# Moving nine FFN products from the output stage of the last phase into its scan loop

## The reference, cut to what matters

```python
xn = layernorm(x)
# branch 1: 16 states for each of 1024 channels, scanned over the tokens
delta = softplus(xn @ Wd.T + bd)
a_bar = exp(-delta * softplus(a_log))
state = a_bar * state + delta * b_param * xn      # over time
y     = state.sum(-1)
# branch 2
real = xn @ cos(theta + theta_noise)
imag = xn @ sin(phi + phi_noise)
out  = x + (y @ Wo.T + bo) + sqrt(real*real + imag*imag)
```

## Time and profile before

| what | value |
|---|---|
| median of the runs | 1132.94 us (2 runs, 1132.84 to 1133.04) |
| the profiled execution | 1131.38 us |
| its span, slowest core (core 3) | 1129.6 us; the eight cores 1123.7 to 1129.6 us |
| VectorE busy | 812.6 us (72%) |
| ScalarE busy | 587.2 us (52%) |
| TensorE busy | 583.5 us (52%) |
| mean granted TensorE clock, core 3 | 0.685 of full speed |

### The profile page before, as it was taken

The page is one execution under the profiler, slowest core; times in us unless marked ns, Lnnn a source line. Parts: engine busy times, 40 slices in busy tenths (PEclk is TensorE's granted clock), DMA queues, the critical chain, the costliest instruction groups (busy, mean ns, idle before and its releaser), DMA issues.

```text
span 1129.6 us, 9385 instructions; the slowest of 8 cores (1123.7 to 1129.6 us)
## 1 busy us (share of the span) xinstructions
PE 583.5 (52%) x2248; PEld 240.7 (21%) x2248; DVE 812.6 (72%) x725; ACT 587.2 (52%) x927; POOL 155.7 (14%) x132
## 2 busy tenths in 40 slices
PE   0423333344467645555544556665565554465685
PEld 0301011111123321221210213443221211121353
DVE  3359788888763348989889984334889989998423
ACT  4575766666643315665555553332465555655430
POOL 2577000000011200000000001221000000000232
PEclk9955555656668856666555666987766556665799
DMA  8877000000002310000000001231100000000023
GB/s 236 228 230 205 2 28 29 28 19 1 0 24 79 111 45 0 1 1 0 1 1 0 1 0 41 87 118 57 42 1 0 0 1 0 1 0 1 28 71 112
DMA packets 36326, 51.67 MB, mean 46 GB/s; under 512 B 3120, under 2 KB 19760, under 8 KB 36272
## 3 DMA queue, kind: packets, MB, share of 16 engines
q1 hardware_dynamic: 33584, 42.68, 13.1%
q0 software_dynamic: 2688, 8.39, 2.1%
HBM read 42.67 MB, written 8.39 MB: 45 GB/s over the span
## 4 chain that ended last, share of the span: by engine, by line
DVE 42%; issue 22%; PE 21%; ACT 10%; POOL 2%; DMA 1%; DVEq 1%; ACTq 0%; POOLq 0%; SPq 0%
DVE grot L722 34%; PE pd L845 6%; PE pt L569 4%; PE pt L579 3%; ACT bdg_bf L171 3%; PE pd L278 3%; DVE sfm L859 2%; ACT abar L676 2%; DVE gcar L733 1%; DMA xsub<-xin 1%; PE pe L357 1%; DVEq L111 1%; PE py L873 1%; ACT L676 1%; DVE xsub L419 1%
## 5 line engine op out<-in xcount | busy, mean ns | idle before, releaser
L722 DVE TENSOR_TENSOR_SCAN grot<-abar,gcar,vbuf 128x768 bf16<-128x768 f32 (+1 forms) x384 | 643.8, 1736 | 69.1 <-ACT abar L676 59.5
L676 ACT ACTIVATE abar<-delta,nega 128x768 f32<-128x768 f32 (+1 forms) x384 | 342.4, 898 | 272.0 <-DVE grot L722 269.0
L760 PE MATMUL pe<-grot,bdg_bf 128*128 128x384 bf16 x256 | 91.6, 460 | 124.8 <-DVE grot L722 124.7
L760 PE MATMUL py<-grot,bdg_bf 128*128 128x384 bf16 x256 | 88.2, 449 | 117.4 <-DVE grot L722 117.4
L278 PE MATMUL pd<-xnbf,wd_bf 128*128 128x384 bf16 (+1 forms) x368 | 97.6, 446 | 18.0 <-ACT xsub L297 14.6
L747 PE MATMUL py<-grot,bdg_bf 128*128 128x512 bf16 x64 | 33.3, 533 | 84.7 <-DVE grot L722 84.7
L619 POOL TENSOR_TENSOR xsub<-r,i 128x384 f32<-128x384 f32 (+1 forms) x9 | 18.1, 2009 | 410.5 <-ACT i L611 410.5
L845 PE MATMUL pd<-ybf,wo_bf 128*128 128x384 bf16 (+1 forms) x320 | 73.3, 379 | 0.0
L747 PE MATMUL pe<-grot,bdg_bf 128*128 128x512 bf16 x64 | 34.3, 543 | 74.9 <-DVE grot L722 74.9
L569 PE MATMUL pt<-xnbf,cos_bf 128*128 128x384 bf16 (+1 forms) x320 | 71.7, 374 | 0.0
L579 PE MATMUL pt<-xnbf,sin_bf 128*128 128x384 bf16 (+1 forms) x320 | 64.8, 347 | 0.0
(11 more groups left out here) (104 smaller groups left out, 565.3 us busy)
## 6 DMA issues: line engine op xcount, KB each, us to landing
xsub<-xin SPq DMA_DIRECT2D x14, 512.0 KB, 4.2
xres<-xin SPq DMA_DIRECT2D x32, 192.0 KB, 2.5
out<-osub POOLq DMA_DIRECT2D x32, 192.0 KB, 2.7
xres<-xin SPq DMA_DIRECT2D x8, 256.0 KB, 3.7
out<-osub POOLq DMA_DIRECT2D x8, 256.0 KB, 3.5
r<-wdt SPq DMA_DIRECT2D x6, 256.0 KB, 6.5
i<-wdt SPq DMA_DIRECT2D x6, 256.0 KB, 6.6
etmp<-tht SPq DMA_DIRECT2D x6, 256.0 KB, 4.5
```

The source lines that it names most:

```text
L676: sx = run("scalar", lambda e, sl=sl_ab, par=par, dt=dt, n=n, tp=tp: e.activation(out=abar[:, sl * TP:sl * TP + tp], in_=delta[:, par * TP ...
L722: vs = run("vector", lambda e, g=gsl, sl=sl_ab, par=par, dt=dt, n=n, tp=tp: e.tensor_tensor_scan(out=grot[:, g * TP:g * TP + tp], data0=ab ...
L760: td = run("tensor", lambda e, c=c, g=gsl, dt=dt, n=n, bb=ypair[c]: e.matmul(bb[:, 0:384], bdg_bf[:, (dt * NST + n) * P:(dt * NST + n + 1) ...
```

## The change

Only phase 2 (the last) changes. All 16 FFN jobs now run in its scan loop, two in each channel tile. Job 2·dt has its matmuls at the top of the tile as before. Its chain, the matmuls of job 2·dt+1 and the chain of that job are entries of `aux`, so they stand behind the exp of consecutive states: behind n = 7, 8 and 9 in tiles 1 to 6, behind n = 5, 6 and 7 in tile 0, and behind n = 3, 4 and 5 in tile 7 (whose `aux` has fewer other entries). The chain at the end of a tile is gone in this phase, and the output stage has no FFN work left. Since the ring's slots in `delta`, `vbuf` and `abar` are in use during the loop, jobs 5 to 15 put their results into `xn32` (the normalised input), into rows that the multiplications of line 333 have already read.

```diff
         NRING = len(ring_ap)
-        ring_stt = [0] * NRING
-        ring_g = [0] * NRING
+        ring_ap = ring_ap + [xn32[:, 512 * s:512 * s + 512] for s in range(12)]
+        ring_stt = [0] * (NRING + 12)
+        ring_g = [0] * (NRING + 12)
...
             def ring_avail_waits(j, eng):
+                if j >= NRING:
+                    s = j - NRING
+                    wait(eng, "V", a_x32_v[p])
+                    wait(eng, "S", a_xnbf_s[p])
+                    for r_ in range((512 * s) // TP, (512 * s + 511) // TP + 1):
+                        wait(eng, vv_done[r_][0], vv_done[r_][1])
+                    return
...
+            P2SLOT = {5: 3, 6: 5, 7: 0, 8: 1, 9: 2, 10: 4,
+                      11: 6, 12: 7, 13: 8, 14: 9, 15: 10}
+
+            def rslot2(i):
+                if p == NPH - 1 and i in P2SLOT:
+                    return NRING + P2SLOT[i]
+                return rslot(i)
...
-            ffn_at = ({6: [0], 7: [1]} if p == 0
-                      else {0: [0], 1: [1], 2: [2], 3: [3], 4: [4],
-                            5: [], 6: [5], 7: [6]})
-            NFC = 2 if p == 0 else 7
+            if p == 0:
+                ffn_at = {6: [0], 7: [1]}
+                NFC = 2
+            elif p == NPH - 1:
+                ffn_at = {dt_: [2 * dt_] for dt_ in range(NDT)}
+                NFC = nch
+            else:
+                ffn_at = {0: [0], 1: [1], 2: [2], 3: [3], 4: [4],
+                          5: [], 6: [5], 7: [6]}
+                NFC = 7
...
+                if p == NPH - 1:
+                    aux.append(("fch", 2 * dt, 0))
+                    aux.append(("fmm", 2 * dt + 1, 0))
+                    aux.append(("fch", 2 * dt + 1, 0))
...
+                        elif kind == "fmm":
+                            emit_ffn_mm(adt)
+                        elif kind == "fch":
+                            emit_ffn_chain(adt)
...
-                for jb in ffn_at.get(dt, []):
-                    emit_ffn_chain(jb)
+                if p != NPH - 1:
+                    for jb in ffn_at.get(dt, []):
+                        emit_ffn_chain(jb)
```

More of the change, by code:

```diff
@@ L596, in rslot @@
                 return i - NRING + 3
+            P2SLOT = {5: 3, 6: 5, 7: 0, 8: 1, 9: 2, 10: 4,
[4 more added lines that the diff above has]
+                return rslot(i)
             def emit_ffn_chain(i):
                 dt, c0, wdth = cjobs[i]
-                j = rslot(i)
+                j = rslot2(i)
                 li = i % 2
@@ L851, in _build @@
                 slot = it % 2
-                jr = rslot(it)
+                jr = rslot2(it)
                 wait("vector", "T", tw)
```

## The result

The changed kernel takes 1140.4 us (median) against 1133.1 before: ratio 1.0067, 95% interval 1.0057 to 1.0077. The ratio leaves out the few executions in which the cores of one die show a lower clock than the others and take longer. The forecast was 1143.5 us with a range of 1132 to 1158, and "within 2%" with a chance of 0.83. So the change makes the kernel slower, as forecast: by 7.3 us, or 0.7%, where 10.6 us, or 0.9%, were forecast.

A forecast was written before the change was run, and what follows sets the result against it. VectorE was taken to bound the phase 2 loop and TensorE the output stage. From 1131.4 us, +29.9 in the loop and −19.5 in the output stage gave 1141.8, or 1143.5 as median; range 1132 to 1158.

The forecast's parts named there:

- Both chains together, 5.15 a tile: Phase 2 loop, tiles 0 to 6: the two mid-tile chains delay scan 10, costing 5.15 us a tile, 36.1 in all.
- the base tile: Phase 2 loop: a tile without losses takes 29.96 us; eight, less 0.38, make 239.3 us.
- 5.68 for the block: Mid-tile in the loop: the second job's 16 matmuls end 5.68 us after scan 7, mostly at the lower clock.
- 4.07 for the rest: After that block: second square, add, Ln, Exp and abar take 4.07 us until scan 10 starts.
- The tile's top, 0.83 each: Start of tiles 1 to 6: VectorE waits for TensorE's states, 0.83 us each, 5.0 in all, between 0.04 and 1.49.
- Tile 7, 6.4: Last tile of the loop: chains at n = 3 to 5 with no vbuf multiplication to cover them lose 6.4 us.
- the 17.6 of before: Phase 2 loop of the kernel before: stalls worth 17.6 us for seven chains, over eight base tiles.
- The output stage: After the phase 2 loop: 54.7 us instead of 74.2, 19.5 shorter, pieces 2.76 apart, three products at the lower clock.
- The rival of a stage that stays at 1.2 GHz: Output stage: the other thirteen products run slow too, 1.31 us each, adding 17.0 for 1160.5 us; chance 0.12.
- The colliding adds: Phase 2 loop: the second add comes while VectorE scans without pause, adding 9.8 us for 1153.3; chance 0.10.
- Hidden altogether: Phase 2 loop: it hides the moved work and today's stalls go too, giving 1096 us, −3.3%; chance 0.03.

The follow-up runs named there:

- e5: Changed kernel with each phase 2 chain cut in two: squares behind one exp, Ln and Exp two states later; 1109.5 us, ratio 0.9786.
- e1: Changed kernel with each tile's second phase 2 chain three states later, its matmuls left in place; 1124.8 us, ratio 0.9935.
- e9: Changed kernel with one job per phase 2 tile, eight in the output stage, and the chain behind n = 12; 1129.0 us, ratio 0.9967.
- e4: Changed kernel with the first job's 16 matmuls moved from the top of tiles 1 to 6 to behind state 2; 1137.7 us, ratio 1.003.
- e10: The split-chain kernel e5 with GpSimd's additions of phase 2 left out; 1099.8 us, ratio 0.9705.
- e6: Changed kernel with three abar slots instead of two in all phases; 1124.9 us, ratio 0.9925, phase 2 loop 294.9 us.
- e2: Changed kernel with one job per phase 2 tile, chain behind n = 7 in tiles 1 to 6, and eight jobs in the output stage; 1134.7 us, ratio 0.9999.
- e8: The split-chain kernel e5 with e4's edit and phase 1's chains split too, all but job 5; 1097.6 us, ratio 0.9674.

## Why the prediction was right

The forecast held because its two terms did: +27.3 in the loop against a forecast of +29.9, and −20.0 in the output stage against −19.5. The mechanism is the forecast one; inside both terms, some smaller errors cancel.

**Both chains together, 5.15 a tile.** Right in place, cause and size: tiles 1 to 6 lost 36.1 us over the base tile, top and chains, against 35.9 in the forecast, and tile 0 lost 5.0 against 5.15. That the two chains share one loss which ends 9.75 after scan 7 was the step that carried it: scan 10 started 9.6 after scan 7's end in tile 4 (967.01 − 957.40), and 9.76 in the mean of tiles 1 to 6. Its two parts, 5.68 for the block and 4.07 for the rest, hold roughly, but only in every second tile. In tiles 2, 4 and 6 the block ended a microsecond earlier (4.70 in tile 4), and the add took a microsecond longer (1.86 to 1.97 instead of 0.98), as it came beside scan 9. The prediction had said in a sentence that these two would about cancel, and they did, within 0.4 us a tile. e5 beside e1 shows that a large part of the loss is ScalarE's standing for the adds, and e1 beside e9 that the wait for the second chain's matmuls is another.

**The tile's top, 0.83 each.** Right: 0.23 to 1.34, together 4.6 for six, and e4 took it away by moving the block. The 0.83 was called the middle of 0.04 and 1.49, which is 0.77; with that the forecast would have been 4.6, too.

**Tile 7, 6.4.** Wrong in size: it lost 3.8. This is the 2.6 by which the loop's term was too large, and it has two parts. Its second block of matmuls (from 1057.37, 1.46 + 1.46) ran at full clock (granted 1.00 from 1057.3 to 1060.2); it came 3 us after the end of the first, where in the middle tiles the second comes some 8 us after the first and begins at the lower level. I had given it the 4.9 us of a block at the lower level. That is 2.0; that the short pause is what kept the clock up, no run tests by itself. The other part, 0.7, is a slip in the sum: tile 7 has no vbuf multiplication (0.38 between scans 7 and 8 instead of 1.06). The 6.4 allowed for that, but the base of eight equal tiles, which the 17.6 of before is counted from, didn't. Against a tile without the multiplication, tile 7 lost 4.4.

**The output stage.** Right, and for the reasons given: three slow products as assumed, pieces 2.69 apart against 2.76 in the forecast. A slow piece cost 1.6 more than a fast one (4.3 against 2.69), not 1.31, since the transposes are slow with it. That there were three slow ones was an assumption, and some luck: in the same execution four of the eight cores had only two, with a stage of 52.6 instead of 54.2. The rival of a stage that stays at 1.2 GHz did not come: after three products with pauses between them the clock rose, and the thirteen that followed, with their own pauses, kept it (granted clock 0.52 before, 1.00 after). The Trainium skill, "TensorE: Matmul & The Clock Gate" (section "A second HAM failure mode: psum-queue depth-cycling"), tells of a clock that goes back and forth between the levels when a kernel pauses between groups of matmuls; the rows of this stage show one rise and no fall.

**The colliding adds** had a chance of 0.10 and a price of 9.8. The mechanism is there, but the price was read wrongly. I took the 2.2 of an add beside scans as an add that runs slowly. It is an add that stands and then runs, and in other places VectorE pays on the other side. In the changed kernel the first chain's add did this in tiles 1 to 7 and the second's in tiles 2, 4 and 6. The forecast had the first one's cost in the row that it took its 2.0 from; the second's, about 1 us, was made up for by the earlier end of the block, so that the full 9.8 did not come. e10 shows what the adds cost once the longer waits are gone.

**Hidden altogether** is what I gave 0.03, because the two slots allow no cover. It did not come, but a third slot is not what it takes (e6: 294.9). The better way is e5's, which needs none, only that nothing that waits for another engine stands between two exps; it leaves 13.3 us of the 44.8.

## What to carry to other kernels

When work moves onto an in-order engine that feeds the bottleneck, count not its busy time but the longest time for which it holds the queue, with the waits inside, and compare that with the number of buffers ahead. A short chain through another engine should be cut at the wait, and its second half put some steps later: here the move lost 7 us with the chain in one piece and gained some 15 with the chain cut and the second job's part put later. And before adding a buffer, ask what the late item waits for last: if it is its own input (e6), the buffer moves the stall and may lengthen it.

## What the runs showed of the hardware that was not expected

GpSimd's two-input add and VectorE's scan (also two inputs from SBUF) hardly overlap. Started in mid-scan the add's record is 1.86 to 2.27 us in the changed kernel, and it ends 0.8 after the scan's end wherever it began (955.91 + 2.27 = 958.18 after 957.40, 962.84 + 1.95 = 964.79 after 964.00). Started between scans or at a scan's very end it is 0.98 to 1.06, and the scan that meets it then mostly takes 2.45 to 2.51 instead of 1.79. A carry copy behind an add takes 0.71 instead of 0.17. Left out (e10), the adds give back 0.57 us each. The Trainium skill, "SBUF — State Buffer" (section "SBUF: two separate sides"), says that the two engines share a port pair, that whichever starts first holds it for its whole instruction, and that VectorE operations with two SBUF inputs are among those concerned. The rows agree with that. The record of a blocked instruction covers the time for which it stands, so that a long add looks like a slow one.

The place of a chain against the scans decides its price: 2.0 behind n = 7 and 1.4 behind n = 12 (e9 against e2, 5.2 us over eight chains), with the same work.

The three transposes of an output piece took 0.87 at the lower clock level and 0.52 at the upper, so these show the level too. How many of the output products ran slow before the clock rose differed between kernels whose output stage holds the same instructions, and also between the cores of one execution: one on every core of e1, two or three in the changed kernel, one or four in e8. In the kernels made from the changed one, the stage took 51.0, 52.6, 54.2 or 55.8 us with one, two, three or four slow products. So a difference of up to 5 us between such kernels can come from this alone.
